# Cross-attention of a decoder block: four kinds of f16 casts put on GpSimd, and TensorE's projections placed between the scores

## The reference, cut to what matters

```python
q = proj(Wq, bq, layernorm(x)); k = proj(Wk, bk, ctx); v = proj(Wv, bv, ctx)   # einsum('oi,bin->bon')
q, k = rotary(q), rotary(k)                       # t * freqs[0] + rotate_half(t) * freqs[1]
scores = einsum('bdhn,bdhm->bhnm', q, k) / sqrt(16)
prob = softmax(scores)
y = einsum('bhnm,bdhm->bdhn', prob, v)
x = x + einsum('oi,bin->bon', Wm, y) + bm
```

## Time and profile before

| what | value |
|---|---|
| time, median of 3 runs | 1810.97 us (1808.18 to 1812.52) |
| profiled execution, its own time | 1800.39 us |
| span of its trace | 1798.6 us |
| mean granted TensorE clock | 0.913 of full speed |
| busy: PE 1469.7, DVE 1069.6, ACT 621.4, POOL 682.7 us | 82%, 59%, 35%, 38% of the span |

### The profile page before, as it was taken

The page is one execution under the profiler, slowest core; times in us unless marked ns, Lnnn a source line. Parts: engine busy times, 40 slices in busy tenths (PEclk is TensorE's granted clock), DMA queues, the critical chain, the costliest instruction groups (busy, mean ns, idle before and its releaser), DMA issues. The chain is left out here.

```text
span 1798.6 us, 28538 instructions
## 1 busy us (share of the span) xinstructions
PE 1469.7 (82%) x9508; PEld 694.1 (39%) x9525; DVE 1069.6 (59%) x1833; ACT 621.4 (35%) x1105; POOL 682.7 (38%) x685
## 2 busy tenths in 40 slices
PE   2689999872478888888888859857999999999988
PEld 1245455440022222222222235424555555556443
DVE  7255565643577888888888654512544454444476
ACT  3223223131146566666666755101111111111121
POOL 6001010014463333332420123671765555667374
PEclk9799999985558999999999978988999999999999
DMA  5656264403381131131120012455666565663465
GB/s 187 188 164 187 72 198 115 156 2 91 70 245 30 42 70 31 42 60 42 30 59 1 1 51 100 166 208 161 168 163 173 146 173 140 180 184 90 128 200 181
DMA packets 197159, 211.25 MB, mean 117 GB/s; under 512 B 90000, under 2 KB 162256, under 8 KB 196688
## 3 DMA queue, kind: packets, MB, share of 16 engines
q1 hardware_dynamic: 167696, 123.67, 26.2%
q0 software_dynamic: 18592, 66.99, 12.0%
q10 hardware_dynamic: 10784, 19.47, 2.9%
HBM read 101.09 MB, written 88.87 MB: 106 GB/s over the span
## 5 line engine op out<-in xcount | busy, mean ns | idle before, releaser
L1015 DVE TENSOR_REDUCE ca_mx<-ca_sc 128x1 f32<-128x512 f32 x512 | 327.9, 678 | 88.8 <-PE ca_sc L935 88.2
L77 PE MATMUL re_ab<-fx_w,re_xt 128*128 x1800 | 295.0, 314 | 36.2 <-DMA re_xt<-slot_rows 36.1
L1155 ACT ACTIVATE ca_pt<-ca_st 128x512 f32<-128x512 f32 x512 | 264.6, 596 | 100.9 <-PE ca_st L947 100.9
L935 PE MATMUL ca_sc<-ca_ks,ca_qs 48*128 48x512 f16 x512 | 186.8, 416 | 53.6 <-DVE ca_mx L1015 31.7
L77 PEld LDWEIGHTS re_ab<-fx_w,re_xt 128*128 128x128 f16 x1800 | 173.2, 98 | 134.1 <-issue 39.3
L947 PE MATMUL ca_st<-ca_qs,ca_ks 49*128 49x512 f16 x512 | 172.5, 400 | 42.7 <-ACT ca_pt L1155 36.8
L77 PE MATMUL re_yp<-fx_w,re_ht 128*128 (+1 forms) x666 | 156.0, 379 | 0.0
L1725 POOL TENSOR_TENSOR fx_w<-re_raw_w,fx_w 128x272 f16<-128x272 f32 x224 | 153.7, 722 | 1.7
L960 PE MATMUL ca_pv<-ca_pt,ca_va 128*32 128x512 f32 x1024 | 148.6, 644 | 1.0 <-DVE ca_turned L1028 0.5
L680 POOL TENSOR_TENSOR sa_yt<-sa_yf,sa_yt 128x512 f16<-128x512 f32 x16 | 18.5, 1156 | 331.0 <-ACT sa_yt L628 331.0
L947 PEld LDWEIGHTS ca_st<-ca_qs,ca_ks 49*128 49x128 f16 x512 | 42.2, 95 | 238.1 <-ACT ca_pt L1155 150.2
(11 more groups left out here) (239 smaller groups left out, 2393.6 us busy)
## 6 DMA issues: line engine op xcount, KB each, us to landing
re_raw_w<-in_we POOLq DMA_DIRECT2D x56, 544.0 KB, 4.7
slot_rows<-sa_zeros SPq DMA_DIRECT2D x12, 1792.0 KB, 15.7
slot_outs<-re_ys ACTq DMA_DIRECT2D x74, 256.0 KB, 2.0
sa_scratch<-sa_qk SPq DMA_DIRECT2D x16, 512.0 KB, 4.0
ca_scratch<-ca_qk SPq DMA_DIRECT2D x64, 128.0 KB, 1.8
sa_qs<-sa_scratch SPq DMA_DIRECT2D x12, 512.0 KB, 6.6
sa_ks<-sa_scratch SPq DMA_DIRECT2D x12, 512.0 KB, 6.9
ca_qs<-ca_scratch SPq DMA_DIRECT2D x48, 128.0 KB, 3.9
```

Of the source, the lines that this page charges most:

```text
L77: last = nc.tensor.matmul(out, lhs(a, c), rhs(b, c), start=(c == 0 and n == 0), stop=(c == chunks - 1 and n == len(PRODUCTS) - 1))
L935: nc.tensor.matmul(sc[:, m % RING, :], qs[rows, c % SLOTS, pair, qt * P:(qt + 1) * P], ks[rows, c % SLOTS, pair, :], start=True, stop=True ...
L1015: nc.vector.reduce_max(mx[:, qd // 4, qd % 4, 2 * a + jj:2 * a + jj + 1], sc[:, m % RING, :], AX.X).then_inc(maxed, 1)
L1155: nc.scalar.activation(pt[:, (4 * qd + k) % 8, :], st[:, m % RING, :], ACT.Exp, scale=SCALE).then_inc(exp_done, 1)
```

## The change: what it does

1. The four kinds of high parts go from ScalarE's activations to `tensor_copy` on GpSimd, each directly ahead of the low part that needs it, in the same steps (`rotated_parts`, `y_parts`, `x_parts`, `c_parts`). Of a full turn these are 4, 4 and 2 casts of 128x512 and one of 128x1024.
2. `split_product` can make a part of its matmuls; q and k projections, values and the second output projection come in halves, the first output projection in thirds, behind the scores of k = 0, of k = 1, or of the whole step.
3. The weighing of the values comes behind k = 2 of its step, not at the step's end.
4. On DVE the turning of the weighed values and the residual come ahead of the step's first maximum.

```diff
+    for m in range(part * total // parts, (part + 1) * total // parts):
+        c, (a, b) = m // len(PRODUCTS), PRODUCTS[m % len(PRODUCTS)]
+        last = nc.tensor.matmul(out, lhs(a, c), rhs(b, c), start=(m == 0), stop=(m == total - 1),
+                                skip_group_check=parts > 1)
...
+                def beside(qd, n):
+                    if projects and qd in (0, 2, 6, 8):
+                        at = n - (0 if qd < 6 else 1)
+                        if at in (0, 1):
+                            project((0, 2, 6, 8).index(qd), e, at, 2)
+                    if ends and qd == 3:
+                        project_out(0, b - 1, n, 3)
+                    if ends and qd == 4 and n:
+                        project_out(1, b - 1, n - 1, 2)
+                    if attend and qd == 7 and n == 2:
+                        turn_maxima(3, b)
+                    if maxima and qd in (5, 9, 13) and n == 2:
+                        turn_maxima(qd // 4 - 1, c)
+                    if maxima and qd in (10, 11, 12, 14) and n:
+                        values((10, 11, 12, 14).index(qd), c, n - 1, 2)
...
-                    if attend:
-                        weigh_values(b, qd)
+                        if k < 2:
+                            beside(qd, k)
+                        if attend and k == 2:
+                            weigh_values(b, qd)
+                    beside(qd, 2)
...
+                    if weighed:
+                        turn_weighed(hq, of)
+                    if ends and qd in (4, 5):
+                        residual(qd - 4, b - 1)
                     if maxima:
                         maximum(c, qd, 0)
-                    if weighed:
-                        turn_weighed(hq, of)
...
-                nc.scalar.activation(yt[:, 0, hq, :], yf[:, hq % 2, :], ACT.Copy).then_inc(y_high, 1)
+            def y_parts(hq, b):
+                pool.wait_ge(norm_done, GROUPS * b + hq + 1)
+                if b:
+                    pool.wait_ge(filled, before["out", b - 1, 1] + 1)
+                nc.gpsimd.tensor_copy(yt[:, 0, hq, :], yf[:, hq % 2, :]).then_inc(y_high, 1)
                 pool.wait_ge(y_high, GROUPS * b + hq + 1)
                 nc.gpsimd.tensor_tensor(yt[:, 1, hq, :], yf[:, hq % 2, :], yt[:, 0, hq, :],
                                         ALU.subtract).then_inc(y_low, 1)
...
                     if projects and qd in (2, 4, 8, 10):
                         roll((2, 4, 8, 10).index(qd), e)
                     if projects and qd in (5, 7, 11, 12):
-                        low_part((5, 7, 11, 12).index(qd), e)
+                        rotated_parts((5, 7, 11, 12).index(qd), e)
                     if ends and qd == 2:
-                        y_low_part(3, b - 1)
+                        y_parts(3, b - 1)
```

More of the change, by code:

```diff
@@ L69, in then_wait, with split_product @@
         self.engine.wait_ge(self.sem, self(instruction))
-def split_product(nc, out, lhs, rhs, chunks):
+def split_product(nc, out, lhs, rhs, chunks, part=0, parts=1):
+    total = chunks * len(PRODUCTS)
     last = None
[L75 to L78, removed]
+    for m in range(part * total // parts, (part + 1) * total // parts):
+        c, (a, b) = m // len(PRODUCTS), PRODUCTS[m % len(PRODUCTS)]
+        last = nc.tensor.matmul(out, lhs(a, c), rhs(b, c), start=(m == 0), stop=(m == total - 1),
+                                skip_group_check=parts > 1)
     return last
@@ L891, in free, with project, values @@
                     pe.wait_ge(emptied, n)
-            def project(u, e):
+            def project(u, e, part, parts):
                 side, oc = u // 2, u % 2
[L896 to L909, removed]
+                if part == 0:
+                    if u == 0:
+                        pe.wait_ge(x_low, 2 * e + 2)
+                    if u == 2:
+                        pe.wait_ge(c_low, e + 1)
+                    free("project", e, u)
+                last = split_product(nc, proj[:, :], lambda a, k: w[:, a, side, k, oc * P:(oc + 1) * P],
+                                     (lambda p, k: xn[:, p, k, :]) if side == 0 else (lambda p, k: cx[:, e % 2, p, k, :]),
+                                     CC, part, parts)
+                if part + 1 == parts:
+                    last.then_inc(filled, 1)
+            def values(kt, c, part, parts):
+                if part == 0:
+                    free("values", c, kt)
+                last = split_product(nc, proj[:, 0:CH], lambda a, k: cx[:, c % 2, a, k, kt * P:(kt + 1) * P],
+                                     lambda p, k: w[:, p, 2, k, :], CC, part, parts)
+                if part + 1 == parts:
+                    last.then_inc(filled, 1)
             def turn_maxima(g, c):
@@ L918, in turn_maxima, with project_out @@
                 last.then_inc(filled, 1)
[L920 to L925, removed]
+            def project_out(oc, b, part, parts):
+                if part == 0:
+                    pe.wait_ge(y_low, GROUPS * b + GROUPS)
+                    free("out", b, oc)
+                last = split_product(nc, proj[:, :], lambda a, k: wm[:, a, k, oc * P:(oc + 1) * P],
+                                     lambda p, k: yt[:, p, k, :], GROUPS, part, parts)
+                if part + 1 == parts:
+                    last.then_inc(filled, 1)
             def score(c, qd, k):
@@ L1112, in split_piece @@
                 nc.scalar.activation(wpair[:, m % 2, 0, 0:n], wraw[:, m % 3, 0:n], ACT.Copy).then_inc(w_high, 1)
[L1114 to L1126, removed]
             def out(u, e):
@@ L1172, in turn @@
                         exponent(b, qd, 3)
-                    if projects and qd in (5, 7, 11, 12):
-                        high_part((5, 7, 11, 12).index(qd), e)
-                    if ends and qd == 2:
-                        y_high_part(3, b - 1)
-                    if attend and qd in (6, 10, 14):
-                        y_high_part(qd // 4 - 1, b)
-                    if pairs and qd == 13:
-                        for j in range(CC):
-                            x_high_part(j, f)
                     if t == -1 and qd >= FIRST_PIECE:
                         split_piece(qd - FIRST_PIECE)
-                if pairs:
-                    c_high_part(f)
             turns(turn)
@@ L1189, in _, with c_parts @@
         def _(pool):
-            def c_low_part(f):
+            def c_parts(f):
+                pool.wait_ge(c_loaded, 16 * f + 16)
+                if f >= 2:
+                    pool.wait_ge(filled, before["values", f - 2, 3] + 1)
+                nc.gpsimd.tensor_copy(cx[:, f % 2, 0, :, :], rawc[:, :, :]).then_inc(c_high, 1)
                 pool.wait_ge(c_high, f + 1)
```

23 lines of the change are left out of this document (13 added, 10 removed).

## The result

The changed kernel takes 1823.84 us (median of 7 runs, 1820.34 to 1840.23) against 1810.97 (7 runs, 1806.40 to 1812.64): ratio 1.0088, 95% interval 1.0059 to 1.0117. It is 12.9 us slower, 16.3 above the forecast and at the upper edge of its range. Another run of it on a second chip gave 1.0128 (1.0082 to 1.0174).

A forecast was written before the change was run, and what follows sets the result against it. DVE was taken as the loaded engine, its idle one wait for scores, 9.0 us a turn. Terms of 1.5 + 1.2 - 2.5 - 2.5 - 2.3 - 0.4 = -5.0 us, 1.5 taken back, gave -3.5: 1807.5 us, range 1784 to 1824.

The forecast's parts named there:

- The casts: Full turn: 11 casts move from ACT to POOL, 0.61 us per 512 columns; unloading ACT is worth nothing by itself.
- The wait for y: Step 3: y comes 5.0 us after the swap, TensorE stands 2.8 us, DVE idles 4.3 against 3.9 before.
- The full turn: Each of turns 1 to 5: terms sum to +0.6 us, less 0.3 for early turning of weighed values, so +0.3.
- Collisions: POOL instructions stretch DVE's: clamp of step 4 +0.7 us; by busy time, an estimated 1.2 us a turn worse.
- Halves behind the last score: Steps 6 and 7: transposed scores wait for ACT behind the evacuation, 2.4 us idle against 2.1; steps 8 to 10 gain 0.8.
- Rival C: Step 3: TensorE's clock halves behind the wait for y, 2.4 us a turn; kernel slower, 1822 us; chance 0.25.
- turns -1 and 0: Two early turns, each forecast 2.5 us shorter; in turn -1 the halves win 3 us in steps 0 to 6.
- start: Turn -2: two rotated casts and the start's x cast join POOL's chain before the first scores, +1.2 us (0.6 to 2.5).
- turns 1 to 5: The five full turns, +0.3 us each, +1.5 us together.
- turn 6: Turn without rotation, so y is not held by `roll`: of 8.5 us idle 2.3 go.
- last turn: Turn 7, in ACT's loop of 2.39 us a step: only the output's parts win, -0.4 us.
- taken back for scatter: Whole kernel: 1.5 us of the gain taken back for POOL's longer queue over 11 moved casts, collisions not placed.

The follow-up runs named there:

- e8: e4 with all four kinds of casts on ScalarE, as before the change; ratio 0.9915 to the kernel before.
- e4: e1 with the maxima's transposes behind k = 1 instead of k = 3 and halves of projections 2 and 3 behind k = 0 and 1; ratio 0.9911.
- profiled run: First profiled execution of the changed kernel, the longest of its seven runs; 1840.23 us, against 1800.39 us for the profiled execution of the kernel before.
- e12: e4 with the values' evacuation at the head of steps 11, 12, 13 and 15 on VectorE; ratio 0.9865 to the kernel before.
- e2: Changed kernel with the four kinds of casts left on ScalarE, y still behind the rotation; ratio 1.0016 to the kernel before.
- second run: Profiled run of the unaltered changed kernel measured again on the chip of the experiments; ratio 1.0128 to the kernel before, cross-attention 665.8 us.
- e7: Changed kernel with the casts on ScalarE and y's low part ahead of the rotation; ratio 0.9954 to the kernel before.
- e9: e8 with only y's casts on GpSimd; ratio 0.9913 to the kernel before.
- e11: Changed kernel with 12 more matmuls on TensorE ahead of the wait for y's low part at step 3; ratio 1.0150 to the kernel before.
- e1: Changed kernel with y's cast and low part ahead of the first rotation in step 2 on GpSimd; ratio 1.0045 to the kernel before.
- e3: Casts on GpSimd, TensorE's and DVE's orders as in the kernel before; ratio 0.9979 to that kernel.
- e6: Casts on GpSimd with y's cast and low part ahead of the rotation, TensorE's and DVE's orders as before; ratio 0.9962 to the kernel before.
- e10: e1 with VectorE's order of before, first maximum ahead of turning the weighed values, residual behind the swap; ratio 1.0098 to the kernel before.

## Why the prediction was wrong

- *The casts*, 0.61 us of 512 columns on POOL: measured 0.61 for y's. The rotated ones take 0.69 on average, the context's 1024 columns 1.04.
- *The wait for y*: PE was to stand 2.8 us and stood 2.75; y was to be there 5.7 us after step 2's first maximum and was; DVE's idle was to be 3.1, 0.7 and 0.4, and is 3.04, 0.60 and 0.36. That chain could be read from the profile of before to a tenth.
- *The full turn*: forecast +0.3 us, measured +0.5 in turn 2 (68.79 against 68.27) and +0.1 in turn 3. *Collisions*: the residual moved ahead leaves the clamp under POOL, as said. DVE is 0.95 us busier. That is nearer to the 1.2 us that I worked out beside the port rule of the Trainium skill's page "SBUF — State Buffer" (section "Who interferes with whom") than to nothing; e8, with the casts on ScalarE, takes 0.87 of it away. It does not decide: e8 and e4 have the same ratio.
- *Halves behind the last score*: steps 6 and 7 idle 2.0 us, forecast 2.4, but step 7 is 1.05 us longer, which e4 takes back. Steps 9 and 10 idle 0.6 less, forecast 0.8.
- **The first step that failed is the price of PE's standing at step 3, "TensorE then stands 2.8 us", taken at full clock.** Rival C had it, and I put its chance at 0.25 against 0.40. Three of five turns in each of the two profiled executions of the change ran the thirds at 1.2 GHz. C's price was too high: 1.5 us a turn, not 2.4, and not in each turn, 4.6 us in all.
- **The second, and the larger one, are the terms for turns -1 and 0: -5.0 forecast, +5.4 measured** in the profiled run and +5.5 in the second, 10.4 and 10.5 us of the miss. I counted bursts there and not the clock. Turn -1 runs wholly at half clock (0.50, before 0.61), so its halves stand between scores at double length. In turn 0 step 6 took 2.2 us more with half clock over it; its length goes from 63.9 (e12) to 73.9 us (e2) over the runs with where the half clock falls, and I can't put it down to a part of the change. Turn -1 takes 63.4 to 64.9 us in all runs with all casts on GpSimd and 61.6 to 64.2 in the others, so the casts may have a share; that is not shown.

| term, us | forecast | profiled run | second run |
|---|---|---|---|
| start | +1.2 | +2.2 | +2.2 |
| turns -1 and 0 | -5.0 | +5.4 | +5.5 |
| turns 1 to 5 | +1.5 | +17.0 | +9.7 |
| turn 6 | -2.3 | -0.8 | -2.2 |
| last turn | -0.4 | +1.1 | +6.1 |
| taken back for scatter | +1.5 | | |
| cross-attention | -3.5 | +24.9 | +21.3 |

- Turns 1 to 5 of the profiled run are 7.3 us above those of the second. Turns 3 and 4 trade places, and the difference is turn 5's, 75.8 us against 68.3: half clock also stands at its steps 12 to 15, which take 22.1 us against 14.7. The second run's excess is in its last turn instead. Why the clock fell in either place is open. The start is the casts, by e2 and e7 to e9.
- The sum has a slip: for steps 6 and 7 it adds 0.1 where the working says 2.4 of idle against 2.1. With 0.3 the five turns come to +2.5. And POOL went to 31.2 us in turn 2, not 30.5, since the context's cast has 1024 columns. Neither decides anything.
- Case C gave 1822 and the median is 1823.84, which is in part luck: C had +13.5 us for turns 1 to 5 and -5.0 for all the rest, and the rest measured +7.9 and +11.6. By the Trainium skill's page "TensorE: Matmul & The Clock Gate" (section "HAM oscillation — how this bites in real kernels"), bursts behind waits run throttled. The trace agrees at 626.90, but in turns 2 and 3 the same stand was followed by full clock; e11 agrees, since filling the wait takes the half clock from the step. That the kernel as a whole gained nothing by it is no part of that section.
- What I had not priced: the values' half of step 12 waits 3.1 us for DVE, where such waits between 600 and 800 us were 1.4 us at most before. e12 puts some 0.5% on it, by its ratio against e4's.

Left open: what lengthened turns -1 and 0 and, in the second run, the last turn; why e1 and e7, which differ by the casts alone, stand 0.9% apart (on two chips) when e4 and e8, which ran on two chips too, don't differ; and what the mean clock of a run follows. e1's ten runs go from 1853.43 us (0.894) to 1869.31 (0.881), and its profile, of the fastest, can't show the slower ones.

## What to carry over

When work is split so that its parts start earlier, ask of each first part what it needs and when that is there: the operand (y), the emptied bank (residual, kept values), and move the producer ahead in its own engine's order in the same edit. A part placed between queued scores turns its own lateness into everybody's. And keep other work of TensorE, here the weighing, between the last part and the next transposed scores (e4): their buffers come free by the same engine that evacuates the part, and without cover the gain of the split goes into that wait.

## What the hardware showed

- TensorE's clock went to 1.2 GHz behind stands of about 2.75 us in three of five otherwise equal turns: the same kernel has steps of 8.20 and 9.74 us side by side. The stretch at half clock behind 626.90 is 3.4 us long. Others are much longer, as this one of e7:
```profile
652.00:672.50 20.50, 19.39 (x80) 3.93 (x81) 12.57 (x25) 11.01 (x20) 5.55 (x4) 0.50 0.31 50
```
  PE was busy 19.39 of the 20.50 us and stayed at half clock.
- Of one kernel, the longer runs mostly have the lower mean granted clock: 0.908 to 0.894 goes with about 20 us (e11), 0.894 to 0.881 with 16 us (e1).
- DVE's divide, 128x256 with both operands in SBUF, has a median of 850 ns in the changed kernel and 848 in e4, but 424 with the old orders and the casts on GpSimd (e3, e6), as with the new orders and the casts on ScalarE (e2, e7, e8). In e10, with VectorE's order of before and all casts on GpSimd, it is 426, and in e9, with y's casts alone on GpSimd, 424. So the divide doubles only where VectorE turns the weighed values early and the other casts are on GpSimd.
